# Causal attention's loop over batch pairs written out on all five engines, with one small memset taken out

## The chip, the cores and the metric

The kernel runs on 1 core of one Trainium2 chip. The metric is the device time of one execution in microseconds (us), the median of several runs. A core has five engines with a queue of instructions each: TensorE (PE; PEld is its weight load), VectorE (DVE), ScalarE (ACT), GpSimd (POOL) and SyncE (SP). They wait for each other by semaphores.

## What is computed

Four residual blocks over an input of 32 batches x 256 tokens x 128 channels, each behind a layer norm. The change touches the first.

```python
x = x + L0_attn(layernorm(x))     # causal attention, 16 heads, q and k of width 128, v of width 8
x = x + L0_ffn(layernorm(x))      # 16 experts, 4 chosen, and a shared one
x = x + L1_attn(layernorm(x))     # attention by hyperbolic distance, 16 heads of width 8
x = x + L1_ffn(layernorm(x))      # relu MLP, width 512

# L0_attn
y = einsum('bnd,hde->bhne', x, Wkqv) + bkqv[None, :, None, :]
k, q, v = y[..., :128], y[..., 128:256], y[..., 256:]
A = einsum('bhnd,bhmd->bhnm', q, k) / sqrt(128)
A = softmax(where(tril, A, -inf))
out = einsum('bhnm,bhmd->bnhd', A, v).reshape(B, N, D) @ Wp + bp
```

## The kernel before, in words

The input stays in SBUF from the first stage to the last. The stages follow each other as blocks of code: `load_and_fold`, `causal_attention`, `moe`, `hyperbolic_attention`, `mlp`. In every block each engine has its own program, written out by hand, and the engines meet through counting semaphores (`wait_ge` waits for a count, `then_inc` adds to it).

`causal_attention` takes the 32 batches two at a time: 16 pairs, numbered from 0. A pair is walked through in 24 slots (`SLOTS`). Three slots make a unit of four heads and one batch; the kind of a slot (s % 3) says which part of the causal triangle its scores are. In a slot

- TensorE makes scores (`pe_scores`, three products of 512 columns, L62 to L64), in four of six slots also the folded queries of one head of what comes next (`pe_fold`, `g_ps`), turns the probabilities of two slots before (`pe_turn`, L486), and at every third slot multiplies by the values (`pe_values`, L499 and L502);
- VectorE adds the mask, takes the negated row maximum of the scores (`dve_max`, L610) and copies turned probabilities of two kinds (L623);
- ScalarE copies `g_ps` to `g_all` (L545), takes the exponential (L553) and copies turned probabilities of the third kind (L620);
- GpSimd splits `g_all` in a rounded part and a rest (`pool_fold`, L566, L567, L590).

Some slots carry more: at slot 5 to 8 the outputs of the pair before are turned back, at 12 they are projected (`pe_project`, L525), at 13 to 15 VectorE takes the statistics for the next layer norm (L650, L654). For the next pair, slot 14 turns the normalised input on TensorE (L440), ScalarE copies it to `xTs` (L534), slot 16 makes the values (L446), and GpSimd splits `xTs` in `x_hi` and `x_lo` (L575) behind its fold of slot 15. Slot 18 holds the first fold of the next pair, which waits for `x_lo`.

`over_turns` (L659 to L672) sets the order over the pairs: pairs 0 and 1 are written out, then a loop (`Fori`, L669) makes 6 iterations of two pairs each, 2 to 13, and pairs 14 and 15 are written out again. In the loop the pair number is a register, so each address and awaited count that depends on it is computed by register instructions on the engine that needs it. In the written-out pairs they are constants.

`dve_max` waits for the scores (`s_ready`) and for the exponential of the slot's buffer (`exp_done`), then clears one spare column of `nmax` (L607), then reduces head by head:

```python
nc.vector.memset(nmax[:, kind, GH:GH + 1], 0.0)
for q in range(heads):
    scores = s_ps[kind][:, q * width:(q + 1) * width]
    last = nc.vector.tensor_tensor_reduce(out=scores, in0=scores, in1=keep.mask[:, N - width:N], ...
```

Nothing reads that column. The reduction is an operation in two instructions, one over the scores and one that reads the accumulated value out.

`hyperbolic_attention`, two stages later, takes 32 batches of 8 head pairs each. Its loop (L1564) has three batches to an iteration, 9 iterations with 8 back edges. VectorE makes `u` (L1513, L1517), GpSimd sums and products of it (L1445, L1456), ScalarE roots (L1418, L1423, L1424), logarithm and exponential (L1432, L1435).

Of the kernel before, what the change touches and what calls it, by code (L numbers as in the profile page):

```python
# [19 lines left out]
P = 128  # L20
# [32 lines left out]
def after(engine, semaphore, count):  # L53

    if isinstance(count, int) and count <= 0:
        return
    engine.wait_ge(semaphore, count)
# [310 lines left out]
def causal_attention(nc, keep, batches):  # L368

    pairs = batches // 2  # L370
    PT = 2 * TB
    W2 = 2 * N
    GH = 4
# [7 lines left out]
    with ExitStack() as stack:  # L381
        m = Names(nc, stack)
# [5 lines left out]
        g_all = m.sb("g_all", [P, 2, W2])  # L388
        g_hi = m.sb("g_hi", [P, 2, GH, W2], F32R)
        g_lo = m.sb("g_lo", [P, 2, GH, W2], F32R)  # L390
        nmax = m.sb("nmax", [P, 3, GH + 1])
        prob = m.sb("prob", [P, 3, 4, P])
        pT = m.sb("pT", [P, 2, GH, 3, P])
        v = m.sb("v0", [P, 2, PT, H, ROWS])
# [32 lines left out]
        def fold_in(p, s):  # L427

            n = s % (3 * 2)
            if n not in FOLD_AT:  # L430
                return None
            h = (s // 6 + 1) * GH + FOLD_AT.index(n)
            return (p, h) if h < H else (p + 1, h - H)


        def pe_turn_x(pe, p):
            pe.wait_ge(xh_done, (p + 1) * PT)
            after(pe, res_done, p - 1)
            for t in range(PT):
                last = nc.tensor.transpose(misc[:, t * P:(t + 1) * P], xh[:, t, :], keep.ident)  # L440
            last.then_inc(xh_turned, 1)
# [159 lines left out]
        def dve_max(dve, p, s):  # L601
            k, kind = p * SLOTS + s, s % 3
            dve.wait_ge(s_ready, k + 1)
            after(dve, exp_done, k - 2)
            heads = GH if kind == 0 else 2
            width = W2 // heads
            nc.vector.memset(nmax[:, kind, GH:GH + 1], 0.0)  # L607
            for q in range(heads):
                scores = s_ps[kind][:, q * width:(q + 1) * width]
                last = nc.vector.tensor_tensor_reduce(out=scores, in0=scores, in1=keep.mask[:, N - width:N], scale=-1.0,  # L610
                                                      scalar=3.4e38, op0=ALU.add, op1=ALU.min,
                                                      accum_out=nmax[:, kind, q:q + 1])
            last.then_inc(max_done, 1)
# [42 lines left out]
        def dve_keep_moments(p):  # L656
            nc.vector.tensor_copy(keep.mv[:, bass.ds(p * PT, PT), :], part_mv[:, :, :]).then_inc(mv_kept, 1)

        def over_turns(engine, body):  # L659


            turns = pairs // 2

            def turn(r, first, last):
                for i in range(2):
                    body(2 * r + i, i, first and i == 0, last and i == 1)
            turn(0, True, turns == 1)
            if turns > 2:
                with engine.Fori(1, turns - 1) as r:  # L669
                    turn(r, False, False)  # L670
            if turns > 1:
                turn(turns - 1, False, True)  # L672

        END = pairs - 1

        with nc.Block() as block:
            @block.tensor
            def _(pe):
                pe.wait_ge(set_up, 1)
                pe_turn_x(pe, 0)  # L680
                pe_make_values(pe, 0)
                for h in range(GH):
                    pe_fold(pe, 0, h, 0)

                def body(p, i, first, last):
                    for s in range(SLOTS):
                        pe_scores(pe, p, s, i)
                        f = fold_in(p, s)
                        if f and not (last and s >= SLOTS - 6):
                            pe_fold(pe, *f, i if s < SLOTS - 6 else 1 - i)  # L690
                        if s >= TURN_LAG or not first:
                            pe_turn(pe, *at_lag(p, s, TURN_LAG))
                        if s % 3 == 0 and (s >= VALUE_LAG or not first):
                            done = at_lag(p, s, VALUE_LAG)
                            pe_values(pe, done[0], done[1] // 3, i if s >= VALUE_LAG else 1 - i)
                        if not first:
                            if BACK_AT <= s < BACK_AT + PT:
                                pe_turn_back(pe, p - 1, s - BACK_AT, p + 1)
                            if s == ATTN_AT:
                                pe_turn_attn(pe, p - 1)  # L700
                            if s == PROJECT_AT:
                                pe_project(pe, p - 1)
                        if not last:
                            if s == XTURN_AT:
                                pe_turn_x(pe, p + 1)
                            if s == VALUES_AT:
                                pe_make_values(pe, p + 1)

                over_turns(pe, body)
                for s in range(SLOTS - TURN_LAG, SLOTS):  # L710
                    pe_turn(pe, END, s)
                for u in range(UNITS - 2, UNITS):
                    pe_values(pe, END, u, 1)
                for t in range(PT):
                    pe_turn_back(pe, END, t, pairs)
                pe_turn_attn(pe, END)
                pe_project(pe, END)

            @block.scalar
            def _(act):  # L720
                for t in range(PT):
                    nc.scalar.activation(xh[:, t, 0:P - 1], keep.x[:, t, 0:P - 1], ACT.Identity, bias=keep.shift_col(t),
                                         scale=keep.rstd_col(t)).then_inc(xh_done, 1)
                act_xT(act, 0)
                act_values(act, 0, 0)
                for h in range(GH):
                    act_fold(act, 0, h)

                def body(p, i, first, last):
                    for s in range(SLOTS):  # L730
                        f = fold_in(p, s)
                        if f and not (last and s >= SLOTS - 6):
                            act_fold(act, *f)
                        act_exp(act, p, s)
                        if s % 3 == 2:
                            copy_turned(act, *at_lag(p, s, TURN_LAG))
                        if not first and s == ATTN_AT:
                            act_attnT(act, p - 1)
                        if not last:
                            if s == XTURN_AT:  # L740
                                act_xT(act, p + 1)
                            if s == VALUES_AT:
                                act_values(act, p + 1, 1 - i)

                over_turns(act, body)
                nc.scalar.preload_act_table_set("sqrt_and_others")
                act_attnT(act, END)

            @block.gpsimd
            def _(pool):  # L750
# [16 lines left out]
                            if s == XTURN_AT + 1:  # L767
                                pool_split_x(pool, p + 1, 1 - i)

                over_turns(pool, body)  # L770

            @block.vector
            def _(dve):
# [30 lines left out]
                        if not last and s == NORM_AT:  # L804
                            dve_norm(dve, p + 1)

                over_turns(dve, body)
                for s in range(SLOTS - TURN_LAG, SLOTS):
                    copy_turned(dve, END, s)
                dve_copy_o(dve, END, GROUPS - 1)  # L810
# [1172 lines left out]
```

## Time and profile before

| | |
|---|---|
| median of 3 runs | 2613.67 us (2610.41 to 2619.83) |
| the profiled execution, its own time | 2611.66 us |
| its span | 2609.8 us |
| instructions in the span | 51267 |
| PE busy | 2134.6 us, 82% |
| DVE busy | 2013.6 us, 77% |
| ACT busy | 1856.5 us, 71% |
| POOL busy | 1645.0 us, 63% |

The stages by the page's slices and the lines' times: the causal attention goes from about 65 to 900 us, the experts to about 1345, the hyperbolic attention to about 2490, the MLP to the end.

How to read it: times are microseconds unless marked ns. An engine's busy time is that of its own operations; register, branch and semaphore instructions are not counted. Matmuls are pipelined and their ends are modelled, so their records overlap. Idle time of an engine is put down to what came last before it went on; "issue" is idle time in which the profile shows nothing that it waited for. The granted clock (PEclk) is TensorE's, as a share of its 2.4 GHz. The DMA queues marked "instruction" bring the engines' own code.

### The profile page before, as it was taken

The page shows a single profiled execution, that of the slowest core. Times are in us where ns is not written, and L with a number is a line of the kernel's source. Part 1 is how long each engine was busy: PE and PEld are TensorE (multiplying, and loading weights), DVE is VectorE, ACT ScalarE, POOL GpSimd, SP SyncE. Part 2 cuts the span into 40 slices and gives each one's busy share as a digit, 9 for nine tenths or more (in the row PEclk, how much of TensorE's full clock was granted, in tenths as well). Part 3 has the DMA queues.
Part 4 walks back from the last instruction along what each step waited for, and adds up shares of the span by engine and source line. Part 5 has one row for each costly group of instructions (what it writes and reads, how often), then busy time and mean ns, then how long its engine had stood idle before and what let it go on. Part 6 is the DMA issues. An engine that isn't in the chain of part 4 may idle for free. (4 is left out here: it accounts for less than half of the span.)

```text
span 2609.8 us, 51267 instructions
## 1 busy us (share of the span) xinstructions
PE 2134.6 (82%) x15144; PEld 1559.0 (60%) x15144; DVE 2013.6 (77%) x6071; ACT 1856.5 (71%) x3189; POOL 1645.0 (63%) x1508
## 2 busy tenths in 40 slices
PE   4999999999999789999966667666666776666599
PEld 3777777777777678888844444444444444433367
DVE  4777777777777666776658998999999899999522
ACT  2766666666676533334328999999999999999743
POOL 3667667777677200000028999999999999999600
PEclk7999999999999889999975666676776657767599
DMA  5000000000000000000000000000000000000011
GB/s 136 2 2 2 1 1 0 1 1 0 1 0 2 1 1 1 0 0 0 1 1 1 1 1 0 0 0 0 0 0 0 0 0 0 0 0 1 1 37 36
DMA packets 25280, 14.83 MB, mean 6 GB/s; under 512 B 2952, under 2 KB 24878, under 8 KB 25166
## 3 DMA queue, kind: packets, MB, share of 16 engines
q1 hardware_dynamic: 16846, 9.36, 1.3%
q10 hardware_dynamic: 8320, 4.19, 0.6%
q8 instruction: 42, 0.69, 0.1%
q14 instruction: 72, 0.59, 0.1%
HBM read 9.36 MB, written 4.19 MB: 5 GB/s over the span
## 5 line engine op out<-in xcount | busy, mean ns | idle before, releaser
L1445 POOL TENSOR_TENSOR u<-u,spare 128x1024 f32<-128x1024 f32 x256 | 597.1, 2375 | 41.6 <-ACT spare L1418 41.6
L553 ACT ACTIVATE prob<-s_ps,nmax 128x128 f32<-128x128 f32 (+1 forms) x1024 | 364.4, 432 | 140.2 <-DVE nmax L610 139.9
L1338 PE MATMUL d_ps<-rowsT 28*128 28x256 f32 x1024 | 171.7, 417 | 326.9 <-DVE u L1517 326.4
L610 DVE CUSTOM_DVE_ANT_0 s_ps<-s_ps,mask 128x128 f32<-128x128 f32 (+1 forms) x1024 | 340.7, 385 | 101.4 <-issue 78.0
L1338 PEld LDWEIGHTS d_ps<-rowsT 28*128 28x128 f32 x1024 | 111.6, 253 | 430.2 <-issue 429.5
L1513 DVE TENSOR_SCALAR u<-d_ps 128x1024 f32<-128x1024 f32 x256 | 311.9, 1218 | 41.7 <-PE i_ps L1338 41.1
L590 POOL TENSOR_TENSOR g_lo<-g_all,g_hi 128x512 fp32r<-128x512 f32 x256 | 329.0, 1285 | 21.4
L1517 DVE SCALAR_TENSOR_TENSOR u<-i_ps,u 128x1024 f32<-128x1024 f32 x256 | 313.5, 1225 | 14.8
L1456 POOL TENSOR_TENSOR spare<-spare,u 128x1024 f32<-128x1024 f32 x128 | 303.1, 2368 | 10.7
L1665 POOL MEMSET rows<- 128x4096 f32 x1 | 3.5, 3512 | 427.8 <-POOLq L352 427.8
L1432 ACT ACTIVATE u<-u 128x1024 f32<-128x1024 f32 x256 | 257.8, 1067 | 0.0
L1435 ACT ACTIVATE u<-u 128x1024 f32<-128x1024 f32 x256 | 257.1, 1062 | 0.0
L1146 ACT ACTIVATE act_g<-eg_ps 128x512 f32<-128x512 f32 x144 | 85.9, 596 | 220.6 <-PE eg_ps L64 220.4
L545 ACT COPY g_all<-g_ps 128x512 f32<-128x512 f32 x256 | 151.6, 592 | 125.8 <-PE g_ps L64 124.8
L1354 PE MATMUL o_ps<-u,v 128*32 128x256 f32 x2048 | 211.2, 552 | 31.7 <-ACT u L1435 31.4
L486 PE MATMUL t_ps<-ident,prob 128*128 128x128 f32 x1536 | 229.9, 272 | 1.6 <-ACT pT L620 1.2
L1326 PE MATMUL r_ps<-ident,rows 128*128 128x128 f32 x1024 | 219.2, 362 | 6.9 <-DVE rows L1508 6.1
L486 PEld LDWEIGHTS t_ps<-ident,prob 128*128 128x128 f32 x1536 | 190.7, 140 | 54.8 <-ACT prob L553 2.0
L1326 PEld LDWEIGHTS r_ps<-ident,rows 128*128 128x128 f32 x1024 | 166.1, 188 | 65.8 <-issue 47.3
L623 DVE COPY pT<-t_ps 128x512 f32<-128x512 f32 x256 | 176.5, 689 | 28.6 <-PE t_ps L486 22.7
L62 PE MATMUL s_ps<-g_hi,x_hi 128*128 128x512 f32 x384 | 185.9, 484 | 3.8 <-POOL g_lo L590 3.8
L566 POOL TENSOR_TENSOR g_hi<-g_all,ones 128x4 fp32r<-128x4 f32 x256 | 51.5, 201 | 194.7 <-ACT g_all L545 191.1
(267 smaller groups left out, 5699.6 us busy)
## 6 DMA issues: line engine op xcount, KB each, us to landing
x<-L_attn_x ACTq DMA_DIRECT2D x8, 512.0 KB, 13.8
y<-y_rows SPq DMA_DIRECT2D x16, 256.0 KB, 2.3
wkqv<-L_attn_Wkqv SPq DMA_DIRECT2D x4, 528.0 KB, 8.6
gate_rows<-L_ffn_gate_proj SPq DMA_DIRECT2D x1, 512.0 KB, 14.5
up_rows<-L_ffn_up_proj SPq DMA_DIRECT2D x1, 512.0 KB, 11.5
down_cols<-L_ffn_down_proj SPq DMA_DIRECT2D x1, 512.0 KB, 12.9
w<-L_ffn_w SPq DMA_DIRECT2D x2, 256.0 KB, 3.0
consts_sb<-consts SPq DMA_DIRECT2D x1, 256.0 KB, 4.4
```

Source lines behind the costliest of these rows:

```text
L486: last = nc.tensor.transpose(t_ps[s % 2][:, c * P:(c + 1) * P], prob[:, s % 3, c, :], keep.ident)
L553: last = nc.scalar.activation(prob[:, kind, at, :].rearrange("p c n -> p (c n)"), s_ps[kind][:, at.start * P:at.stop * P], ACT.Exp, bias=n ...
L590: nc.gpsimd.tensor_tensor(g_lo[:, gb, q, :], g_all[:, h % 2, :], g_hi[:, gb, q, :], ALU.subtract).then_inc(g_split, 1)
L610: last = nc.vector.tensor_tensor_reduce(out=scores, in0=scores, in1=keep.mask[:, N - width:N], scale=-1.0, scalar=3.4e38, op0=ALU.add, op1 ...
L1326: last = nc.tensor.transpose(r_ps[p % 2][:, at:at + P], src, keep.ident)
L1338: last = nc.tensor.matmul(ps[:, e * W2 + j * N:e * W2 + (j + 1) * N], rowsT[at, slot(i, p), 1, j * P:(j + 1) * P], rowsT[at, slot(i, p), 0 ...
L1432: nc.scalar.activation(pair, pair, ACT.Ln, bias=1.0 if whole else 0.0).then_inc(ln_done, 1)
L1435: nc.scalar.activation(pair, pair, ACT.Exp, scale=-1.0 if whole else -2.0).then_inc(w_done, 1)
L1445: nc.gpsimd.tensor_tensor(u[:, slot(i, p), :], u[:, slot(i, p), :], spare[:, p % SPARE, :], ALU.add).then_inc(sum_done, 1)
L1456: nc.gpsimd.tensor_tensor(extra, extra, pair, ALU.mult).then_inc(prod_done, 1)
L1513: nc.vector.tensor_scalar(u[:, slot(i, p), :], d_ps[:, :], 0.0, None, ALU.max).then_inc(dist_done, 1)
L1517: nc.vector.scalar_tensor_tensor(out=u[:, slot(i, p), :], in0=i_ps[:, :], scalar=1.0 / DEN_MIN, in1=u[:, slot(i, p), :], op0=ALU.min, op1= ...
```

## The change

`over_turns` gives way to `over_pairs_of_batches`, a Python loop that writes all 16 pairs out one after the other on TensorE, ScalarE, GpSimd and VectorE (SyncE has no work in this block). Pair number, addresses and awaited counts are constants throughout. The operations and their order in a pair stay as they are. In `dve_max` the memset of the spare column is gone, and `nmax` has no such column any more. Lines behind the change move up by 1 to 10.

```diff
--- before.py
+++ after.py
@@ -388,7 +388,7 @@
         g_all = m.sb("g_all", [P, 2, W2])
         g_hi = m.sb("g_hi", [P, 2, GH, W2], F32R)
         g_lo = m.sb("g_lo", [P, 2, GH, W2], F32R)
-        nmax = m.sb("nmax", [P, 3, GH + 1])
+        nmax = m.sb("nmax", [P, 3, GH])
         prob = m.sb("prob", [P, 3, 4, P])
         pT = m.sb("pT", [P, 2, GH, 3, P])
         v = m.sb("v0", [P, 2, PT, H, ROWS])
@@ -604,7 +604,6 @@
             after(dve, exp_done, k - 2)
             heads = GH if kind == 0 else 2
             width = W2 // heads
-            nc.vector.memset(nmax[:, kind, GH:GH + 1], 0.0)
             for q in range(heads):
                 scores = s_ps[kind][:, q * width:(q + 1) * width]
                 last = nc.vector.tensor_tensor_reduce(out=scores, in0=scores, in1=keep.mask[:, N - width:N], scale=-1.0,
@@ -656,20 +655,11 @@
         def dve_keep_moments(p):
             nc.vector.tensor_copy(keep.mv[:, bass.ds(p * PT, PT), :], part_mv[:, :, :]).then_inc(mv_kept, 1)
 
-        def over_turns(engine, body):
-
-
-            turns = pairs // 2
-
-            def turn(r, first, last):
-                for i in range(2):
-                    body(2 * r + i, i, first and i == 0, last and i == 1)
-            turn(0, True, turns == 1)
-            if turns > 2:
-                with engine.Fori(1, turns - 1) as r:
-                    turn(r, False, False)
-            if turns > 1:
-                turn(turns - 1, False, True)
+        def over_pairs_of_batches(body):
+
+
+            for p in range(pairs):
+                body(p, p % 2, p == 0, p == pairs - 1)
 
         END = pairs - 1
 
@@ -706,7 +696,7 @@
                             if s == VALUES_AT:
                                 pe_make_values(pe, p + 1)
 
-                over_turns(pe, body)
+                over_pairs_of_batches(body)
                 for s in range(SLOTS - TURN_LAG, SLOTS):
                     pe_turn(pe, END, s)
                 for u in range(UNITS - 2, UNITS):
@@ -742,7 +732,7 @@
                             if s == VALUES_AT:
                                 act_values(act, p + 1, 1 - i)
 
-                over_turns(act, body)
+                over_pairs_of_batches(body)
                 nc.scalar.preload_act_table_set("sqrt_and_others")
                 act_attnT(act, END)
 
@@ -767,7 +757,7 @@
                             if s == XTURN_AT + 1:
                                 pool_split_x(pool, p + 1, 1 - i)
 
-                over_turns(pool, body)
+                over_pairs_of_batches(body)
 
             @block.vector
             def _(dve):
@@ -804,7 +794,7 @@
                         if not last and s == NORM_AT:
                             dve_norm(dve, p + 1)
 
-                over_turns(dve, body)
+                over_pairs_of_batches(body)
                 for s in range(SLOTS - TURN_LAG, SLOTS):
                     copy_turned(dve, END, s)
                 dve_copy_o(dve, END, GROUPS - 1)
```

On ScalarE, at slot 14 of a looped pair, which copies the turned input (`xTs`) and the next `g_all`, before:

```order
L553 ACTIVATE prob<-s_ps,nmax 128x256 x2
L57 REGISTER_ALU
L620 COPY pT<-t_ps 128x4x128
L531 REGISTER_ALU
L57 REGISTER_ALU
L534 COPY xTs<-misc 128x512
L543 REGISTER_ALU
L545 COPY g_all<-g_ps 128x512
L549 REGISTER_ALU
L553 ACTIVATE prob<-s_ps,nmax 128x128 x4
```

and with the change:

```order
L553 ACTIVATE prob<-s_ps,nmax 128x256 x2
L619 COPY pT<-t_ps 128x4x128
L534 COPY xTs<-misc 128x512
L545 COPY g_all<-g_ps 128x512
L553 ACTIVATE prob<-s_ps,nmax 128x128 x4
```

The five register instructions between the copies and exponentials are gone; the operations stand in the same order.

On VectorE, at the loop's end, in slot 23 of an odd pair, before:

```order
L623 COPY pT<-t_ps 128x2x256
L603 REGISTER_ALU
L607 MEMSET nmax 128x1
L610 ISA s_ps,nmax<-s_ps,mask 128x256
L610 ISA nmax 128x1
L610 ISA s_ps,nmax<-s_ps,mask 128x256
L610 ISA nmax 128x1
L669 REGISTER_ALU
L669 COMPARE_AND_BRANCH
```

and at a seam of two pairs with the change, up to the first reduction of the next pair:

```order
L622 COPY pT<-t_ps 128x2x256
L609 ISA s_ps,nmax<-s_ps,mask 128x256
L609 ISA nmax 128x1
L609 ISA s_ps,nmax<-s_ps,mask 128x256
L609 ISA nmax 128x1
L609 ISA s_ps,nmax<-s_ps,mask 128x128
```

The memset, the register instruction ahead of it and the branch back are gone; the reductions of the next pair follow at once.

In the built programs VectorE's part of this block grows from 1,532 instructions (446 ahead of the loop, 574 in it, 512 behind it) to 3,488, TensorE's from 2,226 to 5,676, ScalarE's from 935 to 2,268, GpSimd's from 454 to 1,114. VectorE's hyperbolic loop has 315 instructions in both.

## Rows read from the trace of the kernel before

**Rows 1.** The page, busy time and share of the span by engine.

```profile
PE 2134.6 (82%) x15144; PEld 1559.0 (60%) x15144; DVE 2013.6 (77%) x6071; ACT 1856.5 (71%) x3189; POOL 1645.0 (63%) x1508
```

**Rows 2.** Busy time by stretches: stretch, us; engines with counts; granted clock, DMA share, GB/s.

```profile
400.00:500.00 100.00, 98.72 (x748) 76.47 (x747) 76.77 (x372) 69.64 (x179) 70.74 (x104) 1.00 0.00 0
1700.00:1800.00 100.00, 66.90 (x522) 40.70 (x522) 91.07 (x178) 97.20 (x124) 95.66 (x60) 0.69 0.00 0
```

**Rows 3.** Timeline of PE, projection in pairs 1 to 4, 14, 15: start, length.

```profile
142.83 0.49 PE L525 MATMUL misc<-wp,attnT 128*128 128x128 f32 x2
...
194.03 0.49 PE L525 MATMUL misc<-wp,attnT 128*128 128x128 f32 x2
...
245.51 0.49 PE L525 MATMUL misc<-wp,attnT 128*128 128x128 f32 x2
...
297.63 0.49 PE L525 MATMUL misc<-wp,attnT 128*128 128x128 f32 x2
...
814.52 0.49 PE L525 MATMUL misc<-wp,attnT 128*128 128x128 f32 x2
...
865.62 0.49 PE L525 MATMUL misc<-wp,attnT 128*128 128x128 f32 x2
```

**Rows 4.** Waits of PE, 170 to 780 us: total us, times, longest.

```profile
PE g_ps L62 <- POOL x_lo L575: 5.8, 12, 0.5
PE g_ps L62 <- ACT g_all L545: 1.4, 5, 0.4
```

**Rows 5.** Timeline of ACT and PE, slots 15 and 18, pair 1 then pair 5.

```profile
148.28 0.84 ACT L553 ACTIVATE prob<-s_ps,nmax 128x256 f32<-128x256 f32 x2 [0.43 <-DVE nmax L610]
...
154.94 0.50 PE L62 MATMUL g_ps<-x_hi,fold_hi 128*128 128x512 f32 x1 [0.17 <-POOL x_lo L575]
...
354.77 0.84 ACT L553 ACTIVATE prob<-s_ps,nmax 128x256 f32<-128x256 f32 x2 [0.66 <-DVE nmax L610]
...
361.52 0.49 PE L62 MATMUL g_ps<-x_hi,fold_hi 128*128 128x512 f32 x1 [0.48 <-POOL x_lo L575]
```

**Rows 6.** Timeline of DVE at the first back edge, ahead of pair 4.

```profile
269.60 0.14 DVE L610 DVE_READ_ACCUMULATOR2_ANT nmax<- 128x1 f32 x1
271.98 0.06 DVE L607 MEMSET nmax<- 128x1 f32 x1 [2.24 <-issue]
```

**Rows 7.** Timeline of ACT and PE behind that back edge.

```profile
273.24 1.14 ACT L553 ACTIVATE prob<-s_ps,nmax 128x128 f32<-128x128 f32 x4 [1.66 <-DVE nmax L610]
...
274.91 0.50 PE L62 MATMUL g_ps<-x_hi,fold_hi 128*128 128x512 f32 x1 [0.38 <-ACT g_all L545]
```

**Rows 8.** DMA in three stretches: 372 to 475.5, 1560 to 2380, 185 to 186 us.

```profile
q14 instruction: 6, 0.05, 0.1%
...
DMA packets 0, 0.00 MB, mean 0 GB/s; under 512 B 0, under 2 KB 0, under 8 KB 0
...
q14 instruction: 1, 0.01, 3.0%
```

**Rows 9.** Groups by line, the memset; then the timeline of DVE, slot 15, pair 1.

```profile
L607 DVE MEMSET nmax<- 128x1 f32 x384 | 22.7, 59 | 32.1 <-PE s_ps L64 13.3 <-issue 12.3 <-DVE part_stats L650 2.7
...
147.38 0.43 DVE L610 CUSTOM_DVE_ANT_0 s_ps<-s_ps,mask 128x256 f32<-128x256 f32 x1
147.40 0.06 DVE L607 MEMSET nmax<- 128x1 f32 x1
```

**Rows 10.** Timeline of DVE and ACT, last `u` and root of two batches.

```profile
1692.68 1.22 DVE L1517 SCALAR_TENSOR_TENSOR u<-i_ps,u 128x1024 f32<-128x1024 f32 x1
...
1695.19 1.04 ACT L1423 ACTIVATE spare<-u 128x1024 f32<-128x1024 f32 x1
...
2001.31 1.22 DVE L1517 SCALAR_TENSOR_TENSOR u<-i_ps,u 128x1024 f32<-128x1024 f32 x1
...
2002.88 1.05 ACT L1423 ACTIVATE spare<-u 128x1024 f32<-128x1024 f32 x1
```

**Rows 11.** Waits of DVE, 1560 to 2380 us: total us, times, longest.

```profile
DVE u L1513 <- PE i_ps L1338: 26.8, 48, 1.2
DVE rec L1529 <- PE misc L1365: 24.8, 21, 1.2
```

## The prediction

> **What bounds the kernel now.** I read the page first. TensorE is the busiest engine [rows 1], but the share is an average over five stages, so the next view is the busy time by stretches of 100 us [rows 2]. In the stage that the change touches (about 65 to 900 us) TensorE is busy 98.7 of 100 us at a granted clock of 1.00 (2.4 GHz), VectorE 77, ScalarE 70, GpSimd 71: TensorE sets the pace and the others have room. In the hyperbolic stage (about 1350 to 2500) ScalarE has 97 and GpSimd 96 of 100, VectorE 91, TensorE 67: ScalarE and GpSimd set the pace there.
>
> Then the period. Once per batch pair TensorE does the projection of L525, at slot 12, so its start times are a ruler [rows 3]. Pairs 0, 1, 14 and 15 are already written out; 2 to 13 run in the loop, two to an iteration. From pair 14 to 15, both written out, 51.10 us pass. Inside an iteration (2 to 3) it is 245.51 - 194.03 = 51.48, and across a back edge (3 to 4) 297.63 - 245.51 = 52.12. So the trace of before already holds the code of after, with its time: a written-out pair is 0.38 us shorter than a looped one, and a back edge costs some 0.6 us more.
>
> The cause of the 0.38 is in the waits and the timeline. TensorE waits in the loop almost only for `x_lo` of the next pair, 12 times, and 5 times for `g_all` [rows 4]. Its idle time before the fold that reads `x_lo` is 0.17 us in pair 1 and 0.48 in pair 5, and the exponential of slot 15 that stands ahead of this chain on ScalarE waits 0.43 us in the one and 0.66 in the other [rows 5]. The chain is VectorE maximum, ScalarE exponential, copy of `pT`, `xTs`, `g_all`, GpSimd's fold and `x_lo`; register instructions for addresses and counts sit in it, and they alone differ between the two pairs. The remaining 0.07 I give to TensorE's own register work at the seam of two pairs.
>
> The cause of the 0.6 is VectorE. At the back edge it stands still 2.24 us with nothing to wait for that the profile shows ("issue") [rows 6]. ScalarE's exponentials then start 1.66 us late, its `g_all` copy after them, and TensorE gets 0.38 us of idle before the fold [rows 7]; the modelled ends of its matmuls hide the rest of the 0.6. The instruction queue shows why VectorE stands: in one iteration of 103.5 us it moves 6 packets of 8 KB [rows 8], while VectorE runs 574 instructions (counted in the built program). One packet per stretch of 128 instructions, and the first stretch of the loop fetched anew at each back edge: the loop is too long to be held.
>
> **The change, part by part.**
> Loop to straight code. From pair 1's projection to pair 15's are 14 periods in 865.62 - 142.83 = 722.79 us. At 51.10 each they take 715.40. Gain 7.39 us, all on TensorE's path, since every other engine has room. In it are 5 back edges of some 0.6 (3.0) and 12 looped pairs of 0.38 (4.6), which makes 7.6: the same within the rounding.
>
> The fetching of straight code. VectorE's part of this stage grows from 1,532 to 3,488 instructions, TensorE's from 2,226 to 5,676. Pairs 0, 1, 14 and 15 are fetched in just this way, with a packet on the queue [rows 8], and pair 14 to 15 has the shortest period of all: cost 0, between 0 and the 0.6 us of a seam for each of some 15 VectorE stretches more, if a late packet ever held VectorE as the back edge does (9 us). I take 0 because the written-out pairs show it.
> The Trainium skill (Runtime: NRT & Kernel Launch, "Instruction fetch mechanics") says that fetching is sequential and mostly hidden, and that a taken branch to a place no longer held forces a fetch. By that rule the sum is the same, the trace agrees for the 2.24 us, but not for its block of 256 instructions: here 128 go with a packet.
>
> The memset. 384 of 59 ns leave VectorE [rows 9], 22.7 us of work on an engine with 23% to spare, and its wait on `s_ready` goes to the reduction behind it. It counts only where VectorE's maximum is on TensorE's path: the chain of `x_lo`, once for each of the 15 pairs that have a next one, in which the memset of slot 15's neighbours delays the reduction by at most 59 ns, at least by nothing, since the reduction's record starts before the memset has ended [rows 9]. 0 to 0.9 us; I take 0.6, nearer to the whole, because what is hidden is only the dispatch. The remaining idle of 0.17 us can hold a gain of this size. The narrower `nmax` moves no other tile: its 48 or 60 bytes take the same 64.
>
> What moves behind it. The later stages' code is unchanged but lies 1,956 VectorE instructions further on, 36 beyond a multiple of 128. That matters for one loop. The hyperbolic loop has 315 VectorE instructions. In before no packet at all is fetched between 1560 and 2380 us [rows 8]: the loop is held. Counting VectorE's instructions in the trace up to each packet of its straight code (707 at the packet at 185 us, 1,094 at the one at 252 us) puts the borders of the stretches near 64 + 128k, give or take 8, so this loop now starts some 52 into its first stretch and ends at 367, within three (384). After, it starts near 88 and ends at 403, in a fourth. With the next one fetched ahead, five stretches are then wanted. The attention loop, which spans five by itself, was not held; those that span three are. Four is not shown, and I hold it likely (7 in 10) that it is not held: then VectorE stands at each of 8 back edges, as in [rows 6].
> Its price: in [rows 6] about 1.0 us of work was queued ahead of the gap, here it is one `u` operation of 1.22, so the gap is 2.24 - 0.22 = 2.0 us. VectorE has to have `u` ready for ScalarE's root of pair 7; in the batch around 1660 it ended at 1692.68 + 1.22 = 1693.90, a lead of 1.29 us over the root at 1695.19, and in the batch around 2001 at 2002.53 for a root at 2002.88, a lead of 0.35 [rows 10]. Against the 2.0 stand that lead and VectorE's own waits on TensorE, 26.8 + 24.8 us in 24 batches, 2.1 us a batch [rows 11]. If all of these give way nothing is left; if none does, 2.0 pass on, 16 us in 8. I take 0.3 us for each, about 2 us, because the waits alone are as long as the delay.
> By the Trainium skill's page (same section) most engines hold 512 instructions. That is four such stretches, so the fifth would push out the first and the rule has the refetch happen; it gives no price beyond the stall.
>
> Sum: -7.4 - 0.6 + 2 = -6.0 us. The profiled execution took 2611.66 us, so it would take 2605.7; the median of the three runs is 2.01 us above it, and there the forecast is 2607.7. 0.3% of this kernel (7.8 us) is about what a measurement can tell from no change, so this is a real gain under that bound.
>
> **The rivals.**
> Nothing is refetched later (the loop is held over four stretches, or everything is absorbed): -8.0, 2605.7. For it: VectorE's waits in rows 11. Half of this case lies beyond 0.3%, since -8.0 is just at the bound.
> The slower side: the hyperbolic loop is refetched and the delay passes. Place: VectorE's `u` at its 8 back edges; price 2.0 us, up to the 2.24 of the gap itself, so 8 x 2.0 to 8 x 2.24 = 16 to 18 against -8.0: 2621.7 to 2623.7. It decides as soon as the loop spans a fourth stretch and the delay exceeds lead and waits together. For it: a lead of 0.35 us in some batches, and ScalarE without room. Against it: VectorE waits for TensorE in every batch.
> The change doesn't do what it says: straight code of all engines on one queue brings late packets, and the seams return: about 0 in sum, 2613.
>
> **How the numbers follow.** Forecast (attention's gain, small loss later) 0.58; nothing later 0.25; slower side 0.11; late packets 0.06. Low end: -8.0 with the memset at its most, a further 0.3 and 2 us of scatter of a median, 2603. High end: with half of each gap passing on, 8 x 1.0 against 8.0, the time is that of before; 2618 lies between that and the slower case and leaves out under one in ten above. Faster by over 0.3%: half of the second case, a seventh of the forecast's own width, and a little scatter, 0.27. Slower by over 0.3%: the slower side and a remainder, 0.12. The rest, 0.61, within.
>
> **What would show it.** Right: L525's starts are 51.0 to 51.1 us apart in every pair, the idle before the `x_lo` fold is 0.17 us or less, no gap of VectorE at a pair's seam, and the end of the attention comes 8 us earlier. For the later step: packets on the instruction queue between 1560 and 2380 us, five to an iteration, with an "issue" gap of VectorE of about 2 us at each back edge. No such packets mean that four stretches are held. Wrong would be: periods over 51.2, gaps of any engine in the middle of a pair, or a hyperbolic stage longer by over 8 us.

## The result, and the profile after

The kernel with the change takes 2618.3 us, the median of 19 runs (2615.69 to 2620.01); beside it, on the same chip, the kernel before takes 2612.96 (19 runs, 2605.03 to 2619.83). The ratio is 1.0023, with an interval of 1.0015 to 1.0031, and the medians lie 5.3 us apart: slower, where I had forecast a gain of 6. It is the direction of the slower rival, at a price a little under it. The profiled execution took 2618.21 us (span 2616.4), 6.6 more than the one of before.

The page, busy time by engine and the instruction queues (q8 serves TensorE, q14 VectorE; before 42 packets with 0.69 MB and 72 with 0.59 MB). It answers to [rows 1].

```profile
PE 2149.8 (82%) x15144; PEld 1557.6 (60%) x15144; DVE 2008.8 (77%) x5687; ACT 1855.0 (71%) x3189; POOL 1643.8 (63%) x1508
...
q8 instruction: 73, 1.20, 0.2%
q14 instruction: 114, 0.93, 0.1%
```

TensorE has the same matmuls and is busy 15 us longer; VectorE has lost the 384 memsets. The two stretches of [rows 2] say where to look (columns as there):

```profile
400.00:500.00 100.00, 99.68 (x747) 77.86 (x750) 79.12 (x336) 68.59 (x177) 71.43 (x102) 1.00 0.01 2
1700.00:1800.00 100.00, 67.97 (x511) 40.39 (x511) 88.33 (x173) 95.01 (x119) 92.83 (x57) 0.65 0.00 0
```

The attention is a little fuller on TensorE. In the hyperbolic stage ScalarE has fallen from 97 to 95, GpSimd from 96 to 93, and the granted clock from 0.69 to 0.65. So there is a gain in front and a loss behind.

**The gain.** The ruler, timeline of PE, pairs 1 to 4, 14 and 15, as in [rows 3]:

```profile
143.16 0.60 PE L525 MATMUL misc<-wp,attnT 128*128 128x128 f32 x3
...
194.24 0.60 PE L525 MATMUL misc<-wp,attnT 128*128 128x128 f32 x3
...
245.31 0.94 PE L525 MATMUL misc<-wp,attnT 128*128 128x128 f32 x6
...
296.39 0.82 PE L525 MATMUL misc<-wp,attnT 128*128 128x128 f32 x5
...
807.17 0.60 PE L525 MATMUL misc<-wp,attnT 128*128 128x128 f32 x3
...
858.24 0.94 PE L525 MATMUL misc<-wp,attnT 128*128 128x128 f32 x6
```

Each period is 51.04 to 51.11 us, and the 14 together take 715.08 against 722.79: 7.7 us less. Of the 7.2 us that TensorE waited for [rows 4], 2.0 are left, between 170 and 780 us:

```profile
PE g_ps L62 <- POOL x_lo L575: 2.0, 12, 0.2
```

Where VectorE stood still for 2.24 us [rows 6], 0.1 us now pass between the last reduction of pair 3 and the first of pair 4, and its next wait, a slot later, is for an exponential (timeline of DVE, seam of pairs 3 and 4):

```profile
269.07 0.14 DVE L609 DVE_READ_ACCUMULATOR2_ANT nmax<- 128x1 f32 x1
269.31 0.30 DVE L609 CUSTOM_DVE_ANT_0 s_ps<-s_ps,mask 128x128 f32<-128x128 f32 x1
...
270.44 0.69 DVE L622 COPY pT<-t_ps 128x512 f32<-128x512 f32 x1
272.12 0.43 DVE L609 CUSTOM_DVE_ANT_0 s_ps<-s_ps,mask 128x256 f32<-128x256 f32 x1 [0.99 <-ACT prob L553]
```

The first product of the hyperbolic stage, timeline of POOL, comes at 1347.52 us; in the kernel before the same product (L1453 there) came at 1356.14. The gain has grown to 8.6 us by then. It was 7.4 us at the last projection shown (858.24 for 865.62), and what the further 1.2 us are is not shown.

```profile
1347.52 0.20 POOL L1443 TENSOR_TENSOR spare<-u,twos 128x4 f32<-128x4 f32 x1 [17.07 <-DVE u L1507]
```

**The loss.** DMA between 1551 and 2388 us, where [rows 8] shows no packet in the second stretch:

```profile
DMA packets 38, 0.31 MB, mean 0 GB/s; under 512 B 0, under 2 KB 0, under 8 KB 0
...
q14 instruction: 38, 0.31, 0.1%
```

In the window are seven whole iterations with five packets each, as the prediction had it, and three more at its ends. Five packets are what the four stretches that the loop touches and one beyond them would take. The timeline around the first back edge, VectorE, ScalarE and TensorE:

```profile
1546.34 1.21 DVE L1503 TENSOR_SCALAR u<-d_ps 128x1024 f32<-128x1024 f32 x1
...
1549.10 1.22 DVE L1507 SCALAR_TENSOR_TENSOR u<-i_ps,u 128x1024 f32<-128x1024 f32 x1 [1.55 <-issue]
...
1550.47 0.39 PE L1328 MATMUL d_ps<-rowsT 28*128 28x256 f32 x2 [3.06 <-DVE u L1507]
...
1550.91 0.49 PE L1298 MATMUL misc<-ident,xh 128*128 128x128 f32 x2
1551.17 1.21 DVE L1503 TENSOR_SCALAR u<-d_ps 128x1024 f32<-128x1024 f32 x1
1551.52 0.37 ACT L1382 COPY xTs<-misc 128x256 f32<-128x256 f32 x1 [0.98 <-PE misc L1298]
```

VectorE ends a `u` at 1547.55 and starts the next at 1549.10, having waited for nothing that the profile shows. TensorE's pair product (L1328) stands until that `u` has freed its buffer; behind it in TensorE's queue is the turn of the next `x` (L1298), and ScalarE's copy of it is late. The waits from 1551 to 2388 us (total us, times, longest), to be read against the same view of before from 1560 to 2380:

```profile
POOL u L1435 <- ACT spare L1408: 46.3, 24, 4.3
DVE u L1503 <- PE i_ps L1328: 32.0, 48, 1.2
DVE rec L1519 <- PE misc L1355: 24.9, 22, 1.2
...
ACT xTs L1382 <- PE misc L1298: 14.4, 10, 2.9
DVE u L1507 <- issue: 12.1, 7, 1.9
...
ACT rows L1392 <- PE misc L1305: 8.5, 8, 1.3
```

Before, GpSimd waited 31.0 us for ScalarE, ScalarE 5.0 for `xTs` and 3.4 for `rows` behind the products of `misc`. With its third wait on TensorE (`rows` from `r_ps`, 17.1 before, 17.3 after) ScalarE's waits grow by 14.7 us in all, which is the size of the loss that follows. VectorE's own waits are the surprise: 32.0 and 24.9 us against the 26.8 and 24.8 of [rows 11]. I had wanted them to shrink and take up the delay. They have not shrunk at all. From the first product of batch 3 to that of batch 30 (27 periods, all in or beside the loop) 942.5 us pass, before 928.1. The batch behind a back edge takes 35.7 to 37.4 us, the others 33.3 to 34.7.

So 8.6 us are won up to 1350 us, 14.5 lost from batch 3 to batch 30, and 0.7 more lost ahead of and behind that: +6.6, the difference of the two profiled executions.

### The profile page after: what moved, and what is told of

It is laid out like the page before. It is cut to its first block and busy times, and to the rows that moved or that the text cites. A ratio compares the mean times of both kernels' runs of the same rounds, so it can differ in the third digit from the quotient of the medians.

```text
span 2616.4 us, 49025 instructions
## 1 busy us (share of the span) xinstructions
PE 2149.8 (82%) x15144; PEld 1557.6 (60%) x15144; DVE 2008.8 (77%) x5687; ACT 1855.0 (71%) x3189; POOL 1643.8 (63%) x1508
## 5 line engine op out<-in xcount | busy, mean ns | idle before, releaser
L1328 PE MATMUL d_ps<-rowsT 28*128 28x256 f32 x1024 | 176.7, 429 | 325.6 <-DVE u L1507 325.4
L1328 PEld LDWEIGHTS d_ps<-rowsT 28*128 28x128 f32 x1024 | 115.2, 262 | 434.7 <-issue 433.9
L1344 PE MATMUL o_ps<-u,v 128*32 128x256 f32 x2048 | 229.0, 592 | 28.0 <-ACT u L1425 27.8
L1328 PE MATMUL i_ps<-rowsT 6*128 6x256 f32 x1024 | 176.9, 435 | 0.0
```

The costliest lines, as they stand in the source:

```text
L1328: last = nc.tensor.matmul(ps[:, e * W2 + j * N:e * W2 + (j + 1) * N], rowsT[at, slot(i, p), 1, j * P:(j + 1) * P], rowsT[at, slot(i, p), 0 ...
```

## Experiments

In all of them nothing that the kernel computes is left out. "b3 to b30" is the stretch of 27 batches just named. Not all kernels ran on the same chip, so the profiles' stretches carry the argument where the medians can't. The kernel before shows two groups of times on one of the chips, 2608 to 2620 and 2633 to 2644 us (on another, twelve runs of 2611 to 2615 and one of 2627); where its median lies in the upper one, the ratio says little and I give the median itself.

### Where the hyperbolic loop lies in the fetched stretches

`a_pad60`: the change, and 60 one-element memsets that VectorE runs once at the start, so that its later code moves by 60 instructions.

```diff
+        pad = m.sb("pad", [P, 60])
...
+                for n in range(60):
+                    v.memset(pad[:, n:n + 1], 0.0)
                 dve.wait_ge(consts_in, 16)
```

> The change, and 60 memsets of one element each on VectorE at the very start, while it waits for the first load. They move VectorE's later code by 60 instructions, so its hyperbolic loop starts 20 into a stretch of 128 and ends at 335, within three stretches. Theory (the loop's place costs the 15 us): no packets of the instruction queue in the loop, no gap of VectorE at its back edges, batches behind a back edge 34.2 to 34.7 us apart like the others, and a time 8 us below before, about 2605 (ratio 0.997). Rival (TensorE's lower granted clock in the later stages, 0.828 for 0.838, or straight code's fetching, costs the time): the placement changes nothing, 2618 (ratio 1.002).

Measured: 2600.85 us (12 runs, 2598.85 to 2604.19), 17.4 under the change and 4 under what I expected. b3 to b30 takes 925.0. DMA and waits, 1545 to 2375 us:

```profile
q14 instruction: 2, 0.02, 0.0%
...
POOL u L1438 <- ACT spare L1411: 27.7, 24, 2.2
```

Packets, VectorE's gap and the waits of GpSimd behind it are gone together. `b_pad36` is the other way round: the kernel before with 36 such memsets, so that its loop lies as in the change.

> The kernel before, loop and memset kept, with 36 one-element memsets on VectorE at the start: its hyperbolic loop comes to exactly the place that it has after the change (88 to 403 in stretches of 128). Theory: four or five packets to an iteration there, a gap of 1.5 to 2.0 us at each of 8 back edges, and 14 to 16 us more than before (ratio 1.0055 to 1.006). Rival (the clock or straight code): same as before within 0.1%.

Measured: 2649.95 us (6 runs), a median that lies between two groups of three runs, 2635.85 to 2639.05 and 2660.84 to 2663.04. In the profiled run, one of the lower group, 38 packets go to VectorE's queue between 1560 and 2380 us, and b3 to b30 takes 951.1, 23 us more than in before where I had expected 14 to 16; the attention takes 722.82 as in before. The loss comes without any of the change.

`b_pad24` and `b_pad8` (24 and 8 memsets on before) look for the border; `a_pad30` asks whether it was the 60 memsets themselves that helped.

> The kernel before with 24 memsets: the hyperbolic loop at 76 to 391 by my count, 7 instructions into a fourth stretch. Theory (a buffer of four stretches, the next fetched as one is entered): refetched at each back edge like b_pad36, 14 to 16 us more than before. Rival (the loss grows with how far the loop reaches into the fourth stretch, or the border lies elsewhere): no packets and the time of before.

> The kernel before with 8 memsets: the hyperbolic loop at 60 to 375 by my count, 9 instructions short of the fourth stretch. Theory (the border is at 384): no packets in the loop and the batches 34.1 to 34.7 us apart, time of before. Rival (the next stretch but one is fetched before the border is reached, or my count is off by more than 9): refetched as with 24.

> The change with 30 memsets at the start instead of 60: the hyperbolic loop starts 118 into a stretch and ends at 433, over four stretches as in the change itself. Theory (place alone decides): 37 packets in the loop, gaps of about 2 us, 2617 to 2620. Rival (memsets at the start help by themselves, by a warmer or later start): near 2601 or half way.

The place is the loop's, by the count of the prediction, within stretches of 128 instructions of VectorE; the packets are those of VectorE's queue between 1560 and 2380 us:

| kernel | loop at | stretches | packets | b3 to b30 | median (runs) |
|---|---|---|---|---|---|
| before | 52 to 367 | 3 | 0 | 928.1 | 2612.96 (19) |
| b_pad8 | 60 to 375 | 3 | 0 | 928.1 | 2613.62 (10) |
| b_pad24 | 76 to 391 | 4 | 39 | 950.8 | 2660.45 (6) |
| b_pad36 | 88 to 403 | 4 | 38 | 951.1 | 2649.95 (6) |
| change | 88 to 403 | 4 | 37 | 942.5 | 2618.3 (19) |
| a_pad30 | 118 to 433 | 4 | 37 | 948.3 | 2624.76 (4) |
| a_pad60 | 20 to 335 | 3 | 0 | 925.0 | 2600.85 (12) |

With three stretches no packet and 925 to 928 us, with four 37 to 39 packets and 943 to 951, whichever kernel it is and however many memsets: the place decides. The border lies between 375 and 391 by this count, where I had 384. Five of the six runs of `b_pad24` lie at 2659 to 2664 us and one at 2642; its profile is of the upper group, which a later section takes up.

VectorE's gaps add up to 13.3 to 14.1 us in all four kernels with four stretches. Against their counterparts with three, `b_pad24`, `b_pad36` and `a_pad30` lose 23 us, the change 14.5 against before and 17.5 against `a_pad60`. Why the change gets off more lightly is not shown; its granted clock between 1500 and 2380 us is also the highest of the four (0.66 to 0.68 in its parts, 0.61 to 0.66 in the others').

### Is the memset worth anything

`a_memset`: the change with L607 and the spare column put back.

> The change with the memset of the spare column put back (384 on VectorE, three whole stretches of 128, so that the hyperbolic loop lies in the same place as after). Theory: the memset is worth 59 ns on the chain to x_lo once a pair, 15 times, so 0.5 to 0.9 us more than after: period of L525 51.10 for 51.07. Rival (VectorE's 22.7 us are worth more, by earlier exponentials throughout): 3 us or more beyond after.

Measured: 2618.69 us (12 runs, 2615.95 to 2621.42). Periods 51.07, in one pair 51.13; the 14 periods take 714.99 us against 715.08. The memset was worth nothing that can be seen; I had taken 0.6.

### What a stop of VectorE costs the hyperbolic stage

`s_1us` and `s_2us`: `a_pad60`, where no code is fetched again, with a memset of 1.04 or 2.01 us (1173 or 2347 columns) ahead of the first `u` of each of the 9 iterations.

```diff
+        still = m.sb("still", [P, 1173])
...
                     for p in range(HP):
+                        if i == 0 and p == 0 and not isinstance(b, int):
+                            nc.vector.memset(still[:, :], 0.0)
```

> The change with the 60 memsets at the start (hyperbolic loop held), and one memset of about 1.0 us on VectorE ahead of the first u operation of each looped iteration (9 times): the delay of a refetch at half its size, without a fetch. Theory (a delay of u at the batch's start passes on in full, by way of TensorE's turn of x for the next batch, which stands behind it): 9 x 1.0 = 9 us more than the kernel without it (2601), so 2608 to 2610. Rival (my prediction's: the lead of u and VectorE's own waits on TensorE absorb it): under 3 us more.

> The same with a memset of about 2.0 us, 9 times. Theory: 18 us more than 2601, 2617 to 2620, the time that the change has. Rival (lead and waits absorb the first microsecond and the rest passes): 9 us more.

Measured: 2614.77 us (10 runs) and 2629.26 (4 runs); b3 to b30 937.1 and 951.7, so 12.1 and 26.7 more than in `a_pad60`: 1.3 us pass on for each stop of 1.04, and 3.0 for each of 2.01. No slack shows even for the first microsecond, and more comes out than was put in and than I expected. VectorE's own two waits between 1560 and 2380 us, 26.3 and 26.6 us in `a_pad60`, are 32.1 and 23.1 in `s_1us` and 31.4 and 27.1 in `s_2us`: the stops do not use them up. One thing that differs is in the busy times by stretch (last three columns: granted clock, DMA share, GB/s), first `a_pad60`:

```profile
1800.00:2100.00 300.00, 197.22 (x1584) 120.25 (x1583) 273.67 (x532) 292.22 (x371) 287.73 (x178) 0.72 0.00 0
2100.00:2380.00 280.00, 183.97 (x1479) 114.39 (x1478) 256.58 (x489) 273.25 (x345) 269.33 (x164) 0.73 0.00 0
```

then the change:

```profile
1800.00:2100.00 300.00, 202.87 (x1547) 121.83 (x1545) 271.24 (x525) 285.07 (x362) 280.60 (x175) 0.68 0.00 0
2100.00:2380.00 280.00, 189.37 (x1440) 112.84 (x1440) 248.19 (x480) 265.84 (x336) 261.22 (x160) 0.66 0.00 0
```

then `s_1us`:

```profile
1800.00:2100.00 300.00, 209.69 (x1556) 121.00 (x1556) 272.50 (x531) 287.72 (x365) 283.06 (x175) 0.65 0.00 0
2100.00:2380.00 280.00, 199.68 (x1465) 119.19 (x1457) 253.14 (x486) 269.54 (x340) 265.20 (x163) 0.63 0.00 0
```

then `s_2us`:

```profile
1800.00:2100.00 300.00, 211.94 (x1538) 129.40 (x1534) 271.01 (x504) 282.67 (x359) 281.40 (x174) 0.62 0.00 0
2100.00:2380.00 280.00, 196.19 (x1440) 119.34 (x1440) 252.68 (x483) 266.05 (x336) 259.36 (x158) 0.63 0.00 0
```

In all three with stops or gaps the mean granted clock is lower than in `a_pad60`: more of these stretches is spent at 1.2 GHz and less at 2.4. Fewer matmuls (1538 against 1584) take more busy time, and from the fifth iteration on the batches without a stop take 34.4 to 34.7 us in `s_2us` and 34.0 to 34.3 in `a_pad60`. But the clock does not go by the length of the stop: it is as low with 1.04 us (0.65 and 0.63) as with 2.01 (0.62 and 0.63), and higher in the change, whose gaps lie between them. The excess over the stops is 2.7 us in `s_1us` and 8.6 in `s_2us` at nearly the same clock. So the clock can be part of the excess, and what makes up the rest is open; no run holds the clock fixed.

### Which engine's code makes the gain

`m_dve_only` writes out only VectorE (with the 60 memsets), the other three keep `over_turns`; `m_all_but_dve` is the reverse, with L607 kept and no memsets at the start. The edit, for an engine that keeps its loop (here VectorE):

```diff
-                over_pairs_of_batches(body)
+                over_turns(dve, body)
```

> Only VectorE's pairs written out, memset gone, 60 memsets at the start; TensorE, ScalarE and GpSimd keep their loop. Theory (the 0.6 of a back edge is VectorE's, the 0.38 of a pair is register work, mostly ahead of ScalarE's exponential): the back edge's 0.6 gone, period of L525 in the loop 51.3 to 51.4, 3 to 5 of the 7.7 us gained, where TensorE's loop is held. TensorE's own loop can still be refetched as it was with 24 memsets (period 57 at back edges). Rival (back edges cost by TensorE's or ScalarE's own branch): 0.6 stays.

> TensorE, ScalarE and GpSimd written out, VectorE keeps loop and memset (its code and places as before, so the hyperbolic loop is held). Theory: back edges keep their 0.6, the 0.38 of a pair falls to between 0.0 and 0.2; and with no loop on TensorE the long back edges of 5 to 6 us can't come: one mode of times, within 5 us of each other, 2607 to 2611. Rival (the long back edges were VectorE's fetch, not TensorE's): times of 2635 to 2645 in some runs.

Measured: `m_all_but_dve` 2605.97 us (6 runs, 2605.28 to 2607.1), ratio 0.9965 (0.9953 to 0.9978); periods 51.33, and 51.8 to 52.1 at the back edges; b3 to b30 923.4. `m_dve_only` 2636.2 (4 runs), ratio 1.0083 (1.0065 to 1.0101); periods within an iteration 51.25, but 54.9 to 56.4 at the back edges. Of the 0.38 us of a looped pair the other engines' register code thus holds 0.15 (51.48 to 51.33), VectorE's 0.23 (51.48 to 51.25). The excess of 3.7 to 5.1 us at `m_dve_only`'s back edges is the matter of the next experiments.

### TensorE's own loop

`b_pad24` had shown it first. Its attention takes 750.07 us instead of 722.79, and its back edges 56.8 to 57.9. Timeline of PE at one of them:

```profile
382.08 0.79 PE L62 MATMUL s_ps<-g_hi,x_hi 128*128 128x512 f32 x1 [3.53 <-issue]
382.67 0.63 PE L63 MATMUL s_ps<-g_lo,x_hi 128*128 128x512 f32 x1
```

and its busy times, just behind that back edge and 50 us on:

```profile
380.00:390.00 10.00, 7.92 (x39) 5.61 (x40) 3.05 (x16) 2.86 (x9) 2.04 (x3) 0.66 0.01 2
430.00:440.00 10.00, 10.00 (x78) 7.54 (x77) 7.53 (x38) 7.49 (x21) 6.70 (x11) 1.00 0.00 0
```

TensorE stops for 3.53 us and then works at 1.2 GHz for a while: the granted clock is 0.50 from 382 to 387 us and 1.00 again from 388 on, which makes 0.66 in these 10 us. Between 184 and 855 us 53 packets of 16 KB go to its queue, in before 10. `b_pe20` and `b_pe216` move TensorE's code in before by 20 and 216 instructions (40 and 432 waits that are already met, two to an instruction).

```diff
                 pe.wait_ge(consts_in, 16)
+                for _ in range(40):
+                    pe.wait_ge(ident_in, 16)
```

> The kernel before with 20 more instructions on TensorE's queue at the start (waits on a semaphore that has its count). Its attention loop ends 20 instructions further on, past the border of a block of TensorE's code at which it ended before. Theory (the long back edges of 5 to 6 us, seen with 24 memsets and with VectorE alone written out, are TensorE's loop wanting one block too many, and before stands just at that border): long back edges in every run, 16 KB packets throughout the loop, 2636 to 2645. Rival (they come from the chip or from VectorE's timing, not from the place): as before in the same call, 2611 to 2620.

> The same with 216 more, which puts the loop's end 40 instructions ahead of a border. Theory: never refetched, all runs 2608 to 2616, no 16 KB packet in the loop. Rival: as before, with long runs among them if before has them in this call.

Measured: `b_pe20` 2619.84 us (11 runs, 2611.66 to 2636.75); its profiled execution has back edges of 57.6 to 57.8. `b_pe216` 2620.91 (11 runs, 2618.58 to 2623.19), in its profile 10 packets as in before and 722.74 for the attention; its waits themselves cost 11 us at the start (ruler at 154.1 instead of 142.8), and without them it would lie at 2610, within what I expected. It shows one group of times, as expected too. The first missed: I had expected every run to be long, and one of 11 was, the other ten lie at 2611.66 to 2626.49, some of them between the two groups. The profiles of `b_pad24` and `b_pe20` show what a long run is: TensorE's loop is fetched again, and each of 5 back edges costs 5 to 6 us more. By the count of TensorE's instructions in the traces the loop's branch back stands 190 instructions behind a multiple of 256 in before, 212 in `b_pe20` and 150 in `b_pe216`, and the packets of the straight code come mostly at 153 to 254. By this count it ends at a border in the first two and just short of it in the third. What decides in a single run stays open: `m_dve_only` has TensorE's code just as in before, and on a chip on which none of before's 15 runs was long all four of its runs were. With TensorE's loop written out (change, `a_pad60`, `m_all_but_dve`) no run fell in the long group.

### Can the delay be taken off the path by order

`e_early`: the change with TensorE's turn of `x` put ahead of its pair product, and VectorE's residual at the end of the batch before; `e_early_held` is the same with the 60 memsets.

```diff
+                        if one_after and p == 0:
+                            pe_turn_x(pe, b + 1)
                         if following:
                             pe_pairs(pe, *following, i if p + 1 < HP else (i + 1) % TURN)
-                        if one_after and p == 0:
-                            pe_turn_x(pe, b + 1)
```

> The change, with two steps of the hyperbolic stage moved: TensorE turns x for the next batch ahead of its pair product instead of behind it, and VectorE adds the residual at the end of the batch before instead of at pair 0. The loop is still not held. Theory (VectorE's late u reaches ScalarE through TensorE's queue, first by the turn of x): ScalarE's wait for the turned x falls from 14 us to under 3, and 4 to 10 of the 15 us come back, 2608 to 2614. Rival (the delay reaches ScalarE and GpSimd by another way, u itself or the turned rows): 2616 to 2620.

> The same two moves with the loop held (60 memsets at the start). Theory: ScalarE waits only 0.5 us for the turned x there, so nothing or up to 2 us gained beside 2601: 2598 to 2602. Rival: a gain of 3 us or more, as ScalarE's other waits shrink too, or a loss, since the pair product of each batch stands behind the turn.

Measured: 2639.01 and 2625.33 us (11 runs each), 21 and 24 us slower than without the new order, where I had expected a gain; b3 to b30 963.8 and 945.5. Waits of `e_early`, 1551 to 2388 us:

```profile
POOL u L1435 <- ACT spare L1408: 64.5, 23, 5.5
ACT rows L1392 <- PE r_ps L1316: 53.2, 22, 5.3
```

The wait for `xTs` is gone and a longer one for `rows` has come (17.3 us in the change). With the wait for `xTs` gone, the fetched loop still costs 963.8 - 945.5 = 18.3 us, where it costs 942.5 - 925.0 = 17.5 in the old order; VectorE's gaps are longer here, 2.3 to 2.8 us against 1.5 to 1.9. So the copy of `xTs` is not the only way by which the delay gets on. The reading that is left is that `u` on VectorE, the pair product on TensorE and the next `u` on VectorE are a chain without slack, and that ScalarE waits for whatever TensorE does behind that product. It is argued from these waits and from the stops above. The new order costs 20.5 us even with the loop held, and which of its two moves costs them is not shown.

## Why the prediction was wrong

- **Loop to straight code, -7.4: right.** Measured -7.7 over the 14 periods, each 51.04 to 51.11, as pair 14 to 15 of before had shown.
- **Straight code fetched at no cost: right.** Between 70 and 890 us no idle time of VectorE is put to "issue" any more (in before 2.2 us at the longest, ahead of L607), and all periods are alike.
- **The memset, -0.6: mis-sized**, measured 0 within 0.1 us. The idle before the fold that reads `x_lo` stayed at up to 0.2 us.
- **The hyperbolic loop in a fourth stretch is not held: right**, in all four kernels of the table that put it there, with five packets to an iteration and with the gap (1.5 to 1.9 us in the change where I had 2.0). The Trainium skill (Runtime: NRT & Kernel Launch, "Instruction fetch mechanics") states that most engines hold 512 instructions. The runs agree with that figure only if it is counted as four stretches of 128 with one of them for the stretch ahead: the loop of 315 is held where it touches three stretches and not where it touches four.
- **The step that failed is "I take 0.3 us for each, about 2 us, because the waits alone are as long as the delay".** Measured are 1.8 us a back edge against before (14.5 / 8), 2.2 against `a_pad60` (17.5 / 8), and up to 2.9 in the padded kernels of before (23 / 8). VectorE's waits in [rows 11] were no reserve: they were 51.6 us before and are 56.9 after, and `s_1us` shows the same with stops and no fetch. The reading that fits is that VectorE waits there for TensorE, which in that time waits for VectorE's `u`; if the one is late, the other's wait moves along and is not shortened. The lead of [rows 10] was none either. In the trace of after the last `u` of a batch still ends 1.0 to 1.6 us ahead of ScalarE's root in nearly all batches of the loop, as before, and for the first product of a batch the lead of `u` over GpSimd falls from some 7 us to between 4.5 and 5.9 behind a back edge and is back at some 7 one batch later. A lead that is never used up did not keep the others from being late: they waited until VectorE was as far ahead as ever. The granted clock, which I had not in the sum, may have added to it.
- The sign of being wrong that I had named, a hyperbolic stage longer by over 8 us, is what came: some 15.
- **The rival** with this mechanism was at 2621.7 to 2623.7 with a chance of 0.11. The result lies 3.4 us under its low end. 0.8 of these are a smaller loss (15.2 us for 16), with a gap of 1.5 to 1.9 us and more passed on than the gap, 0.6 are a greater gain (8.6 for 8.0), and the other 2.0 are scatter: the median of before came 0.7 lower than in the sum, and the medians differ by 5.3 us where the profiled executions differ by 6.6. It should have had most of the chance once the refetch was held likely; "ScalarE without room" was the argument, and the prediction had it.

The change itself is worth keeping with the loop's place put right: `a_pad60` at 2600.85 us is the fastest of all kernels here, 17.4 us under the change and 12 under before (2612.96, on another chip). On its own chip it lies 11.3 us under the median of the eight runs of before in the lower group (2612.13); the ratio to all 23, 15 of them in the upper group, is 0.9891 (0.9858 to 0.9925).

## What to carry to other kernels

A change in one stage moves the code of all stages behind it. Count where each later loop then begins and ends in the stretches in which its engine's code is fetched, and look at the instruction queue inside the loop; a handful of instructions more or fewer at the start can be worth more than the change. A wait is a reserve only if the engine waited for does not itself wait for the one that is late: follow the circle once round before counting on it, or put a stop of known length in and read what comes out.

## What was not expected of the hardware

- A loop of 315 VectorE instructions runs without a packet where it touches three stretches of 128 instructions, and takes five packets each time round where it touches four.
- A stop of VectorE of 2.01 us, nine times, costs 3.0 us each, with the mean granted clock of TensorE (1800 to 2100 us) falling from 0.72 to 0.62. With half the stop the clock is nearly as low, 0.65, and each stop costs 1.3 us.
- TensorE, when its attention loop is fetched again, stops 3.53 us and then works at a granted clock of 0.50 for some 6 us, so that a back edge costs 5 to 6 us more. One and the same kernel before falls in two groups of times on one chip, some 27 us apart (722.79 in its profile against 750.07 in that of `b_pad24` for the attention), in which a measurement of an unrelated change can easily get lost.
